# A second read of x in feature-major layout, normalised there with rows of mean and root, in place of TensorE's transposes for batches 1 to 7

## What is computed

```python
x = x + layernorm(attn(layernorm(x)))
x = x + layernorm(ffn(layernorm(x)))

def attn(x):                                   # x is normalised
    s    = sigmoid(silu(x @ s_w1.T + s_b1) @ s_w2.T + s_b2)
    u    = (x @ B_w.T + B_b) * s
    h_t  = h_(t-1) @ A.T + u_t                 # a scan over 1024 tokens
    y    = h @ C_w + C_b + x @ D_w.T + D_b
    return y * sigmoid(x @ g_w.T + g_b)

def ffn(x):                                    # squared relu, shared expert
    return square(relu(x @ Ws1)) @ Ws2         # the routed part is zero for these inputs
```

## Time and profile before

| | us |
|---|---|
| median of 3 runs | 879.07 (879.03 to 879.16) |
| the profiled execution's own time | 878.09 |
| its span, first to last instruction | 876.3 |
| busy in the span: PE / DVE / POOL / ACT | 846.2 / 600.0 / 374.5 / 299.5 |

### The profile page before, as it was taken

The page is one execution under the profiler, slowest core; times in us unless marked ns, Lnnn a source line. Parts: engine busy times, 40 slices in busy tenths (PEclk is TensorE's granted clock), DMA queues, the critical chain, the costliest instruction groups (busy, mean ns, idle before and its releaser), DMA issues. The chain is left out here.

```text
span 876.3 us, 12884 instructions
## 1 busy us (share of the span) xinstructions
PE 846.2 (97%) x4120; PEld 699.9 (80%) x4120; DVE 600.0 (68%) x1380; ACT 299.5 (34%) x530; POOL 374.5 (43%) x502
## 2 busy tenths in 40 slices
PE   5999999999999999999999999999999999999985
PEld 3778888888888888888888888888888888888874
DVE  5856775777757778577775777577775767844684
ACT  3431333323432334324342233333343323432333
POOL 0252336254344444253451633616334344435455
PEclk9999999999999999999999999999999999999999
DMA  9320303023220232221232230302323021122112
GB/s 306 127 97 0 97 27 146 21 97 96 95 99 24 73 96 97 98 72 44 77 117 77 96 96 16 144 35 97 96 83 111 3 94 49 49 96 97 49 48 97
DMA packets 17309, 73.23 MB, mean 84 GB/s; under 512 B 2643, under 2 KB 5075, under 8 KB 11094
## 3 DMA queue, kind: packets, MB, share of 16 engines
q1 hardware_dynamic: 17238, 72.38, 23.7%
HBM read 38.82 MB, written 33.55 MB: 83 GB/s over the span
## 5 line engine op out<-in xcount | busy, mean ns | idle before, releaser
L1624 POOL TENSOR_TENSOR xres<-work,xres 128x512 f32<-128x512 f32 x64 | 82.5, 1289 | 62.3 <-DVE work L1196 61.5
L433 PE MATMUL TM<-gw_hi,xT_hi 128*128 128x512 f32 x256 | 104.3, 407 | 0.0
L1588 POOL TENSOR_TENSOR rsz<-rsz,negh 128x1 f32<-128x1 f32 x64 | 39.4, 615 | 149.3 <-DVE rsz L1285 149.3
L433 PE MATMUL TM<-dw_hi,xT_hi 128*128 128x512 f32 x256 | 103.1, 403 | 0.0
L435 PE MATMUL TM<-dw_hi,xT_lo 128*128 128x512 f32 x256 | 100.5, 392 | 0.0
L435 PE MATMUL TM<-gw_hi,xT_lo 128*128 128x512 f32 x256 | 100.5, 392 | 0.0
L434 PE MATMUL TM<-gw_lo,xT_hi 128*128 128x512 f32 x256 | 100.0, 391 | 0.0
L434 PE MATMUL TM<-dw_lo,xT_hi 128*128 128x512 f32 x256 | 99.8, 390 | 0.0
L1588 POOL TENSOR_TENSOR rsv<-rsv,negh 128x1 f32<-128x1 f32 x64 | 35.8, 560 | 122.5 <-DVE rsv L1192 122.5
L1628 POOL TENSOR_TENSOR work<-work,xres 128x512 f32<-128x512 f32 x62 | 79.5, 1293 | 17.5 <-ACT work L908 17.5
L908 ACT ACTIVATE work<-TM,nmz,rsz 128x512 f32<-128x512 f32 x62 | 48.2, 778 | 69.3 <-POOL nmz L1598 69.1
(11 more groups left out here) (146 smaller groups left out, 2071.7 us busy)
## 6 DMA issues: line engine op xcount, KB each, us to landing
xin<-in_x SPq DMA_DIRECT2D x16, 1024.0 KB, 5.6
xres<-in_x SPq DMA_DIRECT2D x16, 1024.0 KB, 5.6
x_scratch<-xres SPq DMA_DIRECT2D x16, 1024.0 KB, 5.3
out<-work SPq DMA_DIRECT2D x30, 512.0 KB, 2.9
xres<-in_g_w_t SPq DMA_DIRECT2D x1, 1024.0 KB, 7.3
xres<-in_D_w_t SPq DMA_DIRECT2D x1, 1024.0 KB, 7.1
work<-in_Ws SPq DMA_DIRECT2D x2, 512.0 KB, 9.5
out<-work SPq DMA_DIRECT2D x4, 256.0 KB, 2.0
```

The source lines that it names most:

```text
L433: eng.matmul(ps, lhs[0], rhs[0], start=first, stop=False)
L1588: return eng.tensor_tensor(dst, src, negh[:, 0:n], ALU.pow)
L1624: eng.tensor_tensor(xres[:, j, :], work[:, j, :], xres[:, j, :], ALU.add).then_inc(S["x1_ok"], 1)
```

## The change

x is also given in a second layout, `x_t`, with features on partitions: for each batch `[p, j, k, c]`, the value of feature 128k + p of row c of tile j. For the batch b + 1 prepared in `body(b)`, the token-major x in `xin` now serves for the statistics alone. Then SyncE writes means and roots of a half (`mv1`, 8 floats for each of 128 partitions) to DRAM, loads the feature-major half over it into `xin` (1 MB), and reads the 1024 floats back into all partitions (`rows_in`, 512 KB). ScalarE sorts them into rows (`rows_apart`), VectorE subtracts the means (`less_mean`) and multiplies by the roots (`scaled`), two tiles at a time, ScalarE writes the ones of feature 0 (`ones_in`), and `ft_hi` and `ft_low` read `xin` where they read PSUM. `FT` stays for batch 0 only. The order on PE, ACT, DVE and POOL is rewritten in `tail` and `body`.

```diff
+            def norm_rows(b, m):
+                js = slice(m * MS, (m + 1) * MS)
+                eng.wait_ge(S["l1_rs"], prep_at("l1_rs", b + 1, m))
+                eng.dma_start(stat_dram[b + 1][m], mv1[:, js, :].rearrange("p j s -> p (j s)")).then_inc(S[f"st_wr{m}"], 16)
+                eng.dma_start(xin[:, js, :], xt[b + 1][:, js, :, :].rearrange("p j k c -> p j (k c)"))\
+                   .then_inc(S[f"xt_ld{m}"], 16)
+                eng.wait_ge(S[f"st_wr{m}"], body_at(f"st_wr{m}", b))
+                if m:
+                    eng.wait_ge(S["rows_ok"], body_at("rows_ok", b, m - 1))
+                eng.dma_start(rows_in[:, :, :].rearrange("p c s -> p (c s)"),
+                              stat_dram[b + 1][m].rearrange("c s -> (c s)").partition_broadcast(P))\
+                   .then_inc(S[f"rows_ld{m}"], 16)
...
                     eng.dma_start(xres[:, js, :], x_v[b][:, js, :]).then_inc(S[f"xres_ld{m}"], 16)
+                    if rep + 1 < NB:
+                        norm_rows(b, m)
...
+            def rows_apart(b, rep, m):
+                eng.wait_ge(S[f"rows_ld{m}"], body_at(f"rows_ld{m}", b))
+                eng.activation(norm_row[:, m, :, :], rows_in[:, :, :].rearrange("p c s -> p s c"), ACT.Copy)\
+                   .then_inc(S["rows_ok"], 1)
+
+            def ones_in(b, rep, m):
+                eng.wait_ge(S["scaled"], body_at("scaled", b, 2 * m + 1))
+                row = xin[0:1, m * MS:(m + 1) * MS, 0:P]
+                eng.activation(row, row, ACT.Identity, bias=one[0:1, :], scale=0.0).then_inc(S["ones_ok"], 1)
...
+            def by_rows(i, row, op):
+                m, s = divmod(2 * i, MS)
+                xT = xin[:, 2 * i:2 * i + 2, :].rearrange("p j (k c) -> p j k c", c=P)
+                r = norm_row[:, m, :, :].rearrange("p (j s) c -> p j s c", s=2)[:, s:s + 2, row, :]
+                return eng.tensor_tensor(xT, xT, r.unsqueeze(2).to_broadcast([P, 2, KD, P]), op)
...
-                low_of(xT_lo[:, j, :, :], ft_bank(rep, j), xT_hi[:, j, :, :]).then_inc(S["ft_lo"], 1)
+                src = first_bank(j)[:, :] if rep < 0 else xin[:, j, :]
+                low_of(xT_lo[:, j, :, :], src, xT_hi[:, j, :, :]).then_inc(S["ft_lo"], 1)
```

More of the change, by code:

```diff
@@ L87, in build @@
         ve1 = sb("ve1", [P, L])
-        rs1 = sb("rs1", [P, L])
+        rows_in = sb("rows_in", [P, P, 2 * MS])
+        one = sb("one", [P, 1])
+        norm_row = sb("norm_row", [P, NM, 2 * MS, P])
         mvv = sb("mvv", [P, L, 2])
@@ L1299, in first_tail @@
                 scan_add(*a, 6)
-                ln1_norm(b + 1, 0)
                 scan_add(*a, 7)
@@ L1353, in body @@
                 attn(*a, 0)
+                less_mean(*a, 0)
+                less_mean(*a, 1)
+                scaled(*a, 0)
                 attn_norm(*a, 0)
@@ L1358, in body @@
                 x1_stats(*a, 0)
+                scaled(*a, 1)
                 x1_stats(*a, 1)
+                hs_low(*a, 3)
+                hs_low(*a, 4)
+                attn(*a, 2)
                 ft_low(*a, 0)
-                attn(*a, 2)
+                less_mean(*a, 2)
                 attn_norm(*a, 2)
                 ft_low(*a, 1)
-                hs_low(*a, 3)
+                attn(*a, 3)
+                ft_low(*a, 2)
+                x1_stats(*a, 2)
                 t_low(*a, 0)
-                attn(*a, 3)
@@ L1367, in body @@
-                x1_stats(*a, 2)
-                ln1_norm(b + 1, 4)
-                hs_low(*a, 4)
-                t_low(*a, 1)
-                ft_low(*a, 2)
-                ln1_norm(b + 1, 5)
-                hs_low(*a, 5)
-                attn_norm(*a, 3)
-                attn(*a, 4)
-                ft_low(*a, 3)
-                x1_stats(*a, 3)
-                hs_low(*a, 6)
+                ft_low(*a, 3)
+                attn_norm(*a, 3)
+                less_mean(*a, 3)
+                attn(*a, 4)
@@ L1379, in body @@
+                x1_stats(*a, 3)
+                hs_low(*a, 5)
+                scaled(*a, 2)
+                h1(*a, 0, 0)
+                hs_low(*a, 6)
+                attn_norm(*a, 4)
+                t_low(*a, 1)
                 attn(*a, 5)
-                hs_low(*a, 7)
-                attn_norm(*a, 4)
-                h1(*a, 0, 0)
                 h1(*a, 0, 1)
+                x1_stats(*a, 4)
+                scaled(*a, 3)
                 t_low(*a, 2)
                 t_low(*a, 3)
-                x1_stats(*a, 4)
+                u_of(*a, 0)
@@ L1387, in body @@
+                hs_low(*a, 7)
                 attn_norm(*a, 5)
-                u_of(*a, 0)
-                ln1_norm(b + 1, 6)
+                ft_low(*a, 4)
+                attn(*a, 6)
+                ft_low(*a, 5)
+                h2(*a, 0, 0)
                 x1_stats(*a, 5)
-                ln1_norm(b + 1, 7)
-                attn(*a, 6)
-                ft_low(*a, 4)
-                ft_low(*a, 5)
+                h2(*a, 0, 1)
                 attn_norm(*a, 6)
-                h2(*a, 0, 0)
@@ L1397, in body @@
-                h2(*a, 0, 1)
+                ft_low(*a, 6)
                 attn(*a, 7)
-                ft_low(*a, 6)
-                x1_stats(*a, 6)
-                attn_norm(*a, 7)
                 ft_low(*a, 7)
                 z_stats(*a, 0)
+                z_stats(*a, 1)
+                attn_norm(*a, 7)
+                x1_stats(*a, 6)
+                h1(*a, 1, 0)
+                x1_stats(*a, 7)
                 t_low(*a, 4)
-                x1_stats(*a, 7)
-                z_stats(*a, 1)
+                t_low(*a, 5)
@@ L1681, in body @@
                 z_rs(b, 0)
-                outs(b, 0)
                 x1_rs(b, 7)
```

206 lines of the change are left out of this document (105 added, 101 removed).

## The result

| | before | after |
|---|---|---|
| median, 20 runs each in turn | 879.21 us | 874.31 us (868.04 to 882.41) |
| ratio | | 0.9926, 95% interval 0.9904 to 0.9948 |
| profiled execution / span | 878.09 / 876.3 | 869.39 / 867.6 |

The ratio leaves out the three longest executions (881.68 to 882.41 us), which lie over 1.5% above the fastest, and without them the median is 872.77 us. So the kernel is 0.7% faster, 6.4 us; it is 4.9 us by the medians of all 20 and 8.7 us by the two profiled executions, where 18.6 us were forecast. The executions of the changed kernel lie 14 us apart, those of the kernel before 4 us.

The account below looks back on a forecast made before the run. PE was taken to bound the loop. The profiled 878.09 us minus 24.6 for transposes plus 6 for PE's waits gave 859.5, so a median of 860.5 us; forecast 856 to 867, full range 852.5 to 877.

Parts of the forecast that it names:

- what leaves PE: Batches 1 to 7 lose 224 transposes of xin on PE, 0.11 us each: 24.6 us, 3.5 us a batch.
- H(0, 0): Early in a body, PE waits here for ft_low(3): 1.4 us late by the sum, 1.0 us a batch taken.
- The 6 us: PE's added waits at H(0, 0) over the six loop batches, taken at 1.0 us a batch.
- The 0.2 us for each meeting with GpSimd: Estimated loss of each VectorE operation with both inputs in SBUF; nine ahead of ft_low(3) make 1.8 us.
- the rows' way: Second half's statistics to DRAM and back as rows: rows_apart done at 19.2 us, less_mean(2) at 20.6, so hidden.
- the cheap end: Lower price for small and broadcast transfers of the rows; with the dear bounds they are done at 23.5, 3 us late.
- Nothing else leaves PE and nothing is added; the scan steps in the tail only change places: On PE, only the 224 transposes go, 24.6 us; the tail's scan steps are merely reordered.
- the floor: Low end of the range, 852.5 us, set 2 us lower for the tail's scan waits.
- rival (b): VectorE-GpSimd interference makes DVE's order bind a body's first 30 us: 3.2 us a batch, 873.5 us; chance 0.19.

Follow-up runs that it names:

- the shorter copy: The changed kernel with VectorE's loop written out, and rows_apart as a plain copy reading one float behind the other (rows not sorted): 847.95 us.
- the written-out kernel: The changed kernel with VectorE's loop over batches 1 to 6 written out six times, without its five jumps: 852.63 us.

## Why the prediction was wrong

**Right: what leaves PE.** "224 x 0.11 = 24.6 us" measured 24.1 us over the seven batches with the jump out of both kernels, small waits on either side included, and a transpose where PE is the bound measured 0.109 us.

**Right, with a term too dear: H(0, 0).** The prediction put `ft_low(3)` at 24.6 us behind `attn(0)` before any loss, added 2.5 us of losses and took 1.0 us a batch for PE. In the trace it is 24.75 us (277.98 to 302.73), losses included, and H(0, 0) starts at 302.96. The 6 us are a few tenths a batch: the shorter copy gives back 3.3 us over the seven. The 0.2 us for each meeting with GpSimd did not fall on VectorE (1225 and 687 ns, nothing over the rows); GpSimd's sums became longer, which PE did not notice.

**Right: the rows' way.** From attn(0), which the prediction put 3.5 us into the body: the statistics of the second half are issued 6.3 us in (forecast 4.6), the rows 11.8 (12), `rows_apart` ends 20.9 (19.2), 1.1 us of that since it is twice as long as the plain copy, and `less_mean(2)` starts at 20.9 (20.6), having waited 0.88 us for it:

```profile
280.82 0.33 SPq L376 DMA_DIRECT2D ln_scratch<-mv  x1
...
286.23 0.35 SPq L382 DMA_DIRECT2D rows_in<-ln_scratch  x1
...
293.18 2.17 ACT L880 ACTIVATE norm_row<-rows_in 128x1024 f32<-128x1024 f32 x1
...
295.38 1.22 DVE L1178 TENSOR_TENSOR xin<-xin,norm_row 128x1024 f32<-128x1024 f32 x1 [0.88 <-ACT norm_row L880]
```

The broadcast lands in 5.4 us, and these statistics in no more than 5.4 (280.82 to 286.23), where the prediction took 7.5 us with the queue: the cheap end, as chosen. That the rows go out when forecast is luck, an issue 1.7 us later and a landing 2.1 us faster.

**Wrong: the tail.** The step that failed is "Nothing else leaves PE and nothing is added; the scan steps in the tail only change places", with the floor that let the tail's waits of 2 us go. VectorE's tail was read for what it does, not for what stands first in it. The rows that it needed were in the trace of before: five waits for carry, 2.6 us in all, and `scan_add(0)` 2.45 us idle at the head of every pass. That reads as a wait for PE, and it hid a standstill of about the same length that ended just then: with the statistics put first in that same kernel, VectorE stood 2.3 to 2.4 us ahead of them. In the changed kernel the jump costs 20.8 us over the seven batches in place of 5.5, made up of 15.3 us of waits and 4.7 to 5.1 us of clock. The difference is 15.3 us too, by chance the same figure, and 24.1 - 15.3 = 8.8 us is what the profiled execution keeps (721.5 - 712.7). Executions with a lower mean clock keep less.

None of the rivals was this one. The time lies in the range of rival (b), 867 to 877 us, but that is luck: VectorE does the same work in the written-out kernel, and the loss is gone. Its meetings with GpSimd and its order cost some tenths of a microsecond a batch, not the 3.2 us of (b). The direction and size of the loss at the jump were open to the prediction: 1 us of statistics ahead of an operation that PE waits for five times already.

## What to carry to other kernels

What stands first behind a loop's jump has the jump's standstill ahead of it: keep the operation that the critical engine waits for there only if the other engine's work covers it, put nothing before it, or write the loop out. A wait that the profile puts down to the other engine may hide a second one of its own that ends a moment earlier, so ask of each operation that is moved ahead of it what it would then push. And when work leaves the bound engine, look for what that work had covered: here 24 us left PE, and with the old order and the loop kept 11 came out.

## What the chip showed that I had not expected

- VectorE's jump back over a whole batch's instructions stood still for 2.4 to 3.1 us and then 1.2 to 1.5 us (2.3 to 2.4 and 2.4 to 2.7 us in the kernel before with the statistics first), with three instruction packets more each; a jump over a few instructions did not.
- PE's granted clock fell to its lower level behind three of five gaps of about 3 us in one execution, and behind all five in another kernel with gaps of up to 4.0 us; behind gaps of up to 1.2 us it did not. A gap cost up to 1.7 us more than its length. One kernel with such gaps spread by 14 us over 20 executions, in step with its mean clock; two others with such gaps spread by 3 us over five.
- 4 KB stored in pieces of 4 bytes landed in 9.2 to 13.9 us; in pieces of 32 bytes in 1.4 us, or 5.2 to 5.8 us right behind a load of 1 MB.
